# A first layer norm of two row groups computed one stage earlier, and fewer spare matrix products at the start of the next stage

## What is computed

```python
def _layernorm(x, axis=-1, eps=1e-05):
    m = jnp.mean(x, axis=axis, keepdims=True)
    v = jnp.var(x, axis=axis, keepdims=True)
    return (x - m) / jnp.sqrt(v + eps)

# sublayer 1: state-space layer (a scan over time), then residual and norm
x = _layernorm(x + _L0_attn_ref(x, ...), axis=-1)
# sublayer 2: x1 = _ln(x, ln1_g, ln1_b), then self attention on x1
x = _layernorm(x + _L0_xattn_ref(x, ctx_512, ...), axis=-1)

def _ln(x, g, b):
    m = jnp.mean(x, -1, keepdims=True)
    v = jnp.var(x, -1, keepdims=True)
    return (x - m) * jax.lax.rsqrt(v + 1e-05) * g + b
...
x = _ln(xx, ln1_g, ln1_b)          # the norm that the change moves for 8 of 64 sequences
x = x + _mha(x, x, ...)            # which begins with xn = _ln(x, lnx_g, lnx_b)
```

## Time and profile before

| | us |
|---|---|
| median of 3 runs | 3524.48 |
| lowest, highest | 3520.35, 3525.49 |
| the profiled execution: its own time | 3520.38 |
| its span in the trace | 3518.5 |
| PE busy | 3132.9 (89%) |
| DVE, ACT, POOL busy | 2410.5, 1967.9, 2064.2 |
| mean granted TensorE clock | 0.959 of full speed |

### The profile page before, as it was taken

The page is one execution under the profiler, slowest core; times in us unless marked ns, Lnnn a source line. Parts: engine busy times, 40 slices in busy tenths (PEclk is TensorE's granted clock), DMA queues, the critical chain, the costliest instruction groups (busy, mean ns, idle before and its releaser), DMA issues. The chain is left out here.

```text
span 3518.5 us, 101747 instructions
## 1 busy us (share of the span) xinstructions
PE 3132.9 (89%) x40973; PEld 1931.2 (55%) x40973; DVE 2410.5 (69%) x5699; ACT 1967.9 (56%) x3510; POOL 2064.2 (59%) x1842
## 2 busy tenths in 40 slices
PE   6888888877999999898999999999999989999676
PEld 2433444433555556665666666665555545666575
DVE  5999999994555555585665556677888855666465
ACT  5666666652566666432666654335555536666354
POOL 5888888884787877663111114556777742343365
PEclk8999999998999999998999998999999989999798
DMA  4222222225600000000000000000000000000364
GB/s 143 103 90 91 96 100 92 89 88 195 217 2 2 2 2 2 16 1 13 4 5 5 5 3 6 8 8 2 2 2 2 2 17 24 21 17 14 98 175 116
DMA packets 50327, 165.42 MB, mean 47 GB/s; under 512 B 11822, under 2 KB 23217, under 8 KB 40784
## 3 DMA queue, kind: packets, MB, share of 16 engines
q1 hardware_dynamic: 45520, 150.43, 13.1%
q0 software_dynamic: 4352, 8.47, 0.7%
HBM read 149.89 MB, written 43.65 MB: 55 GB/s over the span
## 5 line engine op out<-in xcount | busy, mean ns | idle before, releaser
L530 DVE TENSOR_TENSOR_SCAN XC<-ssm_dA,ssm_db 128x2048 f32<-128x2048 f32 x128 | 565.2, 4416 | 55.6 <-PE ssm_db L374 55.6
L479 ACT ACTIVATE ssm_dA<-ssm_delta,ssm_nega 128x508 f32<-128x508 f32 x512 | 326.0, 707 | 165.9 <-DVE XC L530 162.6
L1229 POOL TENSOR_TENSOR self_pm<-self_pT,weights 128x512 f32<-128x512 f32 x256 | 322.6, 1294 | 54.4 <-ACT self_pT L953 53.0
L594 POOL TENSOR_TENSOR XC<-XC,XB 128x1536 f32<-128x1536 f32 x64 | 253.3, 3958 | 87.9 <-DVE XC L530 87.9
L1235 POOL TENSOR_TENSOR XC<-XC,XB 128x128 f32<-128x128 f32 x128 | 58.5, 458 | 391.6 <-DVE XB L1111 391.6
L594 POOL TENSOR_TENSOR ssm_hC<-XC,XB 128x1536 f32<-128x1536 f32 x64 | 251.8, 3934 | 36.6 <-DVE XC L530 36.6
L374 PE MATMUL ssm_db<-XB,ssm_dxT 32*128 32x128 f32 x4096 | 157.0, 292 | 103.3 <-DVE XC L530 88.9
L374 PEld LDWEIGHTS ssm_db<-XB,ssm_dxT 32*128 32x128 f32 x4096 | 131.7, 193 | 203.8 <-DVE XC L530 183.9
L1097 DVE TENSOR_REDUCE self_nmax<-self_scores 128x4 f32<-128x512 f32 x256 | 158.0, 679 | 82.0 <-PE self_scores L830 81.8
L2663 POOL TENSOR_TENSOR XC<-XC,weights 128x512 f32<-128x512 f32 x128 | 161.8, 1285 | 73.1 <-ACT XC L2497 73.1
L2671 POOL TENSOR_TENSOR XC<-XC,weights 128x512 f32<-128x512 f32 x128 | 161.4, 1283 | 49.7 <-ACT XC L2506 49.5
(11 more groups left out here) (454 smaller groups left out, 8354.3 us busy)
## 6 DMA issues: line engine op xcount, KB each, us to landing
XB<-c_rows SPq DMA_DIRECT2D x64, 1024.0 KB
sorted<-in_padding SPq DMA_DIRECT2D x1, 33280.0 KB, 109.2
experts_we<-in_w_experts SPq DMA_DIRECT2D x72, 323.0 KB, 3.1
experts_rt<-sorted SPq DMA_DIRECT2D x72, 65.0 KB
ssm_xT<-in_xT SPq DMA_DIRECT2D x16, 256.0 KB
XC<-in_w_experts SPq DMA_DIRECT2D x9, 256.0 KB
weights<-in_w_self SPq DMA_DIRECT2D x1, 1412.0 KB, 7.3
cross_ctx_t<-in_ctx SPq DMA_DIRECT2D x16, 77.0 KB
```

The source lines that it names most:

```text
L479: o = act.activation(dA[:, p % 2, :].rearrange("p (b k t) -> p b k t", b=GROUP, k=4)[:, :, k, 1:T], by_batch(delta[:, slot, half, :])[:, : ...
L530: dve.tensor_tensor_scan(states(p).rearrange("p m t -> p (m t)"), dA[:, p % 2, :], db[:, :], 0.0, ALU.mult, ALU.add).then_inc(h_ready, 1)
L594: pool.tensor_tensor(weighted(p).rearrange("p (b k) t -> p b k t", k=4)[:, :, 0:3, :], states(p).rearrange("p (b k) t -> p b k t", k=4)[:, ...
L1229: pool.tensor_tensor(pm[:, n % 2, r, :].rearrange("p (h t) -> p h t", h=4), pT[:, n % 2, r, :].rearrange("p (h t) -> p h t", h=4), bcast(V ...
```

## The change

In the last step of the state-space phase, where the group index is NG, three pieces are added. DVE takes the row statistics of X for groups 0 and 1 (`next_rows`, part 0). ACT normalises these rows from X into XC (`next_norm`, part 0) once the last readers of XC's states are done. POOL computes the reciprocal deviations and shifts and applies gain and offset (`next_inverse`, `next_spread`, part 1). In self attention the same work is taken out for groups 0 and 1, and each engine raises the semaphores by the amount that the removed work raised. The spare products ahead of the transposes go from 9 to 2, and those ahead of the first q product from 2 to 1.

```diff
@@ ssm_phase, ACT, in step(g, slot) @@
                         elif more(g):
                             decay(g + 1, 1 - slot, 0)
+                    elif p == 0:
+                        next_norm()
...
+            def next_norm():
+                act.wait_ge(hC_dve, NG * U)
+                act.wait_ge(hC_pool, NG * U)
+                for n in range(2):
+                    act.wait_ge(next_step, 4 * n + 4)
+                    for b in range(GROUP):
+                        o = act.activation(XC[:, n * GROUP + b, :], X[:, n * GROUP + b, :], ACT.Identity,
+                                           scale=next_rstd[:, n, b:b + 1], bias=next_shift[:, n, b:b + 1])
+                    o.then_inc(next_normed, 1)
@@ ssm_phase, DVE @@
+                    if p == 0 and not there(g):
+                        next_rows()
...
+            def next_rows():
+                dve.wait_ge(x_out, 2)
+                for n in range(2):
+                    row_stats(dve, lambda b: X[:, n * GROUP + b, :], next_stats[:, n], next_mv[:, n], next_vec, n * VEC, mark)
@@ ssm_phase, POOL @@
+                    if p == 1 and not there(g):
+                        pool.wait_ge(env["weights"]["self"][1], 16)
+                        for n in range(2):
+                            next_inverse(n)
+                        for n in range(2):
+                            next_spread(n)
...
+            def next_inverse(n):
+                pool.wait_ge(next_vec, (n + 1) * VEC)
+                pool.sem_inc(mark, 1)
+                inv_std(pool, power[:, :], next_mv[:, n], next_rstd[:, n], next_step, 4 * n)
+                pool.wait_ge(next_step, 4 * n + 2)
+                pool.tensor_tensor(next_shift[:, n], next_mv[:, n, :, 0], next_rstd[:, n], ALU.mult).then_inc(next_step, 1)
+                pool.wait_ge(next_step, 4 * n + 3)
+                pool.sem_inc(mark, 1)
+                pool.tensor_scalar(next_shift[:, n], next_shift[:, n], -1.0, None, ALU.mult).then_inc(next_step, 1)
+
+            def next_spread(n):
+                gain, offset = env["self_vectors"]
+                rows = XC[:, n * GROUP:(n + 1) * GROUP, :]
+                pool.wait_ge(next_normed, n + 1)
+                pool.sem_inc(mark, 1)
+                pool.tensor_tensor(rows, rows, bcast(gain, 1, GROUP), ALU.mult).then_inc(next_step, 1)
+                pool.wait_ge(next_step, 2 * n + 9)
+                pool.sem_inc(mark, 1)
+                pool.tensor_tensor(rows, rows, bcast(offset, 1, GROUP), ALU.add).then_inc(next_step, 1)
@@ wide_attention_phase, PE @@
-            keep_warm(pe, ob, ident, 9 if own else 3)
+            keep_warm(pe, ob, ident, 2 if own else 3)
...
-                        keep_warm(pe, ob, ident, 2)
+                        keep_warm(pe, ob, ident, 1)
@@ wide_attention_phase, ACT @@
             if own:
-                x1_norm(0)
+                act.sem_inc(x1_normed, 2)
                 in_norm(0)
-                x1_norm(1)
@@ wide_attention_phase, DVE @@
             if own:
-                x1_stats(0)
+                dve.sem_inc(vec, 2 * GROUP)
+                in_stats(0)
...
             dve.tensor_copy(pick[:, :, :], bcast(sel, 2, P)).then_inc(folded, 1)
...
             dve.memset(nsplit[:, :, :], 0.0).then_inc(folded, 1)
-            if own:
-                in_stats(0)
-            else:
+            if not own:
...
             if own:
-                x1_stats(1)
+                dve.wait_ge(vec, VEC)
+                dve.sem_inc(vec, 2 * GROUP)
             in_stats(1)
@@ wide_attention_phase, POOL @@
             if own:
-                x1_inv(0)
-                x1_spread(0)
+                pool.sem_inc(pool_step, 5)
+                pool.sem_inc(x1_ready, 1)
             in_inv(0)
             if own:
-                x1_inv(1)
-                x1_spread(1)
+                pool.wait_ge(pool_step, POOL)
+                pool.sem_inc(pool_step, 5)
+                pool.sem_inc(x1_ready, 1)
             in_inv(1)
```

6 lines of the change are left out of this document (added).

## The result

The changed kernel takes 3511.63 us, median of nine runs (3501.21 to 3516.74). The kernel before, measured beside it, takes 3521.94, also of nine (3512.50 to 3525.91). The ratio of the two is 0.9972, with a 95% interval of 0.9960 to 0.9984: 9.9 us faster, between 5.6 and 14.1. The forecast was 3511.6, 12.9 us faster. Time and sign were right, and the gain came out some 3 us smaller than forecast, a difference that lies inside the interval. That the forecast time was hit to 0.03 us is luck: the forecast started from 3524.48 for the kernel before, whose median of nine is 2.5 us lower, and this made up for the smaller gain.

What follows compares the result with a forecast made beforehand. At the seam into self attention, the first norm through DVE's queue and then spare products delay PE in series. Starting the first q product 12.9 us earlier, all else zero, gives 3524.48 - 12.9 = 3511.6 us, range 3504 to 3519.5.

Steps and rivals of the forecast that it cites:

- What bounds the seam: Start of self attention: first norm through DVE's queue up to 841.91, then spare products, in series set the first q product.
- Part 1: Last state-space step: added DVE, POOL and ACT work hidden in idle time, phase end unmoved; POOL overrun 0, range 0 to 2.1 us.
- POOL still in the gain and offset when DVE's last statistics are done: Last state-space step: a sign, named beforehand, that would show the forecast wrong.
- Part 2: Start of self attention: without the norm, bias copies start behind PE's product, spare products at 836.16 instead of 841.91, 5.75 us.
- Part 3: Fewer spare products: first q product at 840.8 or 841.45 against 854.12, 13.3 or 12.7 us earlier; 12.9 taken.
- my bounds of 3.25 and 4.51: Delay in us from the start of dense PE work to the rise of the granted clock, read from two places.
- The low level did not reach q and k: Rival at the q and k products: low clock through all eight costs 6.9 us, products before 0.8; 3519.3; chance 0.10.
- The slower case: Rival in the first attention beats: PE stays at 1.2 GHz, loss 20.1 us with group 1, 3531.7; chance 0.04.
- Only the spare products count: Rival at the seam: PE doesn't wait for the first norm, fewer spare products alone give 6.9 us, 3517.6; chance 0.03.
- The clock doesn't fall at the seam: Rival at the barrier: clock stays up, first q product at 838.4, 15.7 us earlier, 3508.8; chance 0.05.
- Part 4: Attention loop after the first q product: earlier start carries through; low clock stretches plus or minus 3.2 us, taken as zero.
- The sum: Whole kernel: median 3524.48 - 12.9 = 3511.6 us, profiled execution 3507.5 us.

Runs made afterwards that it cites:

- norm_only: The change with nine and two spare products as before, so only the norm is moved: median 3517.76 us, ratio 0.9992 to before.
- products_only: The kernel before with two and one spare products instead of nine and two, norm not moved: median 3515.36 us, ratio 0.9990.
- changed: First profiled execution of the changed kernel, with no further edit: 3516.01 us; median of the kernel 3511.63 us, ratio 0.9972 to before.
- changed_again: The changed kernel once more without edit, for a second profile: profiled 3500.75 us, median 3511.18 of 12, ratio 0.9977 to before.
- tail_only: The change with eight instead of six spare products at the end of the state-space phase: median 3504.37 us, ratio 0.9968 to before.
- tail_two_late: The change with eight spare products in the tail, and DVE applying the second group's gain and offset after POOL's last norm: median 3502.22 us, ratio 0.9955.
- tail_eight: The change with the second group's gain and offset on DVE, eight spare products in the tail, none at the start: median 3500.62 us, ratio 0.9946.
- pad_late: The change with the 33 MB padding transfer issued after the sixteenth sequence's score products: median 3509.73 us, ratio 0.9974 to before.

## Why the prediction was right, step by step

**What bounds the seam: right, with one wait overlooked.** Two things stood in series, the norm through DVE's queue and the spare products. Removing one alone brings the first beat forward by 4.8 or 4.6 (`norm_only`), 3.3 or 4.9 (`products_only`), both by 11.4. That spare products also covered ACT's copy behind the second group's norm was not in the forecast; the change takes this wait away by its other half, which was luck.

**Part 1, POOL: the term was zero where it depends on the clock.** I set its overrun at 0, with 0 to 2.1 kept. POOL's times were right, but not the time at which DVE would want it. When the last products run at the higher level (3.66 us) the inverse is 1.4 us late (`changed`); at the lower one (5.34) it is on time (`changed_again`). One of my own signs of being wrong, POOL still in the gain and offset when DVE's last statistics are done, so appeared in that trace. Besides, 0.4 us went at the barrier, which I had not foreseen. The price of both can be read. Timelines of DVE and PE, before, and of DVE, changed:

```profile
805.99 4.42 DVE L530 TENSOR_TENSOR_SCAN XC<-ssm_dA,ssm_db 128x2048 f32<-128x2048 f32 x1 [0.57 <-PE ssm_db L374]
814.55 5.90 PE L389 MATMUL ssm_y<-ssm_hC,weights 64*64 64x512 f32 x32 [5.04 <-POOL ssm_hC L594]
```

```profile
804.81 4.42 DVE L547 TENSOR_TENSOR_SCAN XC<-ssm_dA,ssm_db 128x2048 f32<-128x2048 f32 x1 [1.48 <-PE ssm_db L379]
```

From the start of the last scan to the barrier, less the time of the last products, it is 19.2 us before (831.09 - 805.99 - 5.90), and the same in the three other traces with the old tail. It is 21.0 in `changed` (829.44 - 804.81 - 3.66) and in the two others whose POOL was late, and 19.6 in `changed_again` (832.74 - 807.79 - 5.34) and the three others where it was on time. So the term cost 1.8 or 0.4 us, inside the 0 to 2.1 that I kept.

**Part 2, the bias products: the mis-sized term.** I took L762 to end 4.05 us after PE's start as before, so the copies at 835.3, 4.1 behind the barrier. The copies came at 835.06, but only because the barrier was earlier. Measured from it, L812 ended 5.6 us behind it (832.97 + 2.06 - 829.4), instead of 4.15 (before). PE had stood idle for 3.97 us at the barrier instead of 2.21, 2.60 in `changed_again`, and the clock fell within a microsecond of the barrier, not after 1.6. Stretch of the changed kernel:

```profile
829.00:830.00 1.00, 0.44 (x3) 0.47 (x3) 0.12 (x1) 0.48 (x1) 0.10 (x1) 0.74 0.03 8
```

All the one-column products then run at the lower level. That is 1.4 us and makes the step from 12.9 to 11.4 in this trace. In `changed_again` the clock fell 0.7 us behind the barrier, the bias products cost 0.9 us more than forecast, and the late rise of the clock the other 0.5. With two more products ahead of the barrier it comes back: `tail_only` and `tail_two_late` have first beats 1.7 and 1.6 us earlier than the change, and in `tail_eight` the bias products end 3.0 us behind the barrier.

**Part 3, fewer spare products: right in the steps, helped by luck in the times, and one bound too narrow.** Spare products at 835.94 (forecast 836.2), transposes at 839.51 (839.6), the first q product at 841.00 (840.8 to 841.5), the first scores at 849.51 (849.3 to 850). These times agree because the barrier came 1.7 us earlier, which hides the 1.4 of part 2. From the first spare to the first q product it was 5.06 us, within my 4.6 to 5.3. The clock rose 3.8 us after the spare products began, between my bounds of 3.25 and 4.51:

```profile
839.00:840.00 1.00, 1.00 (x5) 0.48 (x4) 0.00 (x0) 0.00 (x0) 0.92 (x2) 0.64 1.29 426
```

In `changed_again` it rose after 5.0 us, above the upper bound, and 5.57 us lay between the two. Two values were too few to bound a delay that differs from execution to execution.

**The rivals.** The low level did not reach q and k: 3.92 us for eight records of q, as before (3.85). With no spare products at all it did, and cost 1.5 us (2.8 in `tail_eight`), not 6.9. The page of the Trainium skill that I had set against the change, "TensorE: Matmul & The Clock Gate", asks in its section "Why this matters for your kernels" to keep TensorE busy without a break for full throughput. The three spare products that are left were enough for that here. The slower case, the low level through the first beats, did not come: the clock was at 1.00 from 839.7 to 860.2 in the changed kernel. "Only the spare products count" fell with `products_only`: its 6.9 us would have been 3.3 to 4.9, for ACT's queue was in the way. "The clock doesn't fall at the seam" did not happen either in the change; the three kernels with eight products in the tail come near to it.

**Part 4, carrying through: right in the mean, and the spread was real.** The loop kept 12.50 and 11.77 of its lead. I allowed plus or minus 3.2 for low stretches. Between the first and the eleventh beat the leads grew by up to 2.3 us (`tail_eight`) and shrank by up to 4.4 (`norm_only`), so the allowance was near the truth. But I had put it down to the clock only. The stops of PE of up to 3.1 us during the transfer are the other part, and stood in the trace of before (2.20 at 902.49).

**The sum.** Self attention became 12.4 us shorter in one trace and 11.7 in the other (624.0 less 611.6 and 612.3), against 12.9. The state-space phase varies by itself: with its old code it took 829.9 to 831.8 in four traces (mean 830.8), with the change's code 829.4 to 834.3 in six (mean 832.2). The means differ by 1.4 us, less than twice what four and six values so scattered leave uncertain. Part 1 shows what the change does there: 0.4 or 1.8 us more behind the last scan. What differs ahead of the scan is code that the change leaves alone. My forecast was that the phase would end where it did. The barrier behind self attention came 14.1 us earlier in one trace (1441.0) and 10.1 in the other (832.7 + 612.3 = 1445.0). The median says 9.9, interval 5.6 to 14.1. The 0.4 or 1.8 us of the tail would explain most of the 2 us between this and the shorter self attention, but this is not shown, since later phases vary by more (`cross` 525.4 to 533.7, `narrow` 441.9 to 452.6 over all traces).

The best version by its median is `tail_eight`, 0.9946 (0.9930 to 0.9962) of before, about 19 us. It is clearly faster than before. Against the change (0.9960 to 0.9984 in one comparison, 0.9964 to 0.9989 in the other) the intervals just overlap or just don't, and the two never ran beside each other, so an advantage of some 10 us is likely but not shown. The traces account for 3 to 4 us of it in self attention (608.8 against 611.6 and 612.3), and the first beat for less than 1.

## What to carry to other kernels

Spare products and a serial chain that cover each other must be removed together, and whatever else they covered has to be looked for on every engine's queue: here a copy on ACT behind another group's norm. Count times at a seam from the barrier: the times on the trace's own clock agreed with the forecast by the luck of an early barrier. Look at what TensorE did ahead of it. Its idle time there is not all that decides at which level the first products run: `tail_only` idled 2.27 us and `products_only` 2.21, yet the clock fell 3.1 and 0.9 us behind the barrier, with eight and six products in the tail. Compare phases, not whole traces, when an effect is 0.3%: unchanged phases differed by 8 to 11 us.

## What the runs showed of the hardware that was not expected

- During a large transfer (33 MB, DMA share about 1.0) and just at its end TensorE stands for 0.2 to 3.1 us at a time with nothing that the profile shows to wait for; when the transfer was issued later, the stops came later (0.21 and 2.56 us in `pad_late`). They stand at places of TensorE's instruction list that lie multiples of 256 records apart. Stops of up to 0.7 us stand elsewhere too, at a smaller DMA share (before, 0.69 at 3275.5, share 0.20).
- Two more wide products ahead of a barrier held the granted clock at 1.00 until 3.1 to 3.9 us behind it, over products of one column; with the shorter row and 3.97 us of idling it fell within 0.1 us of the barrier.
- POOL's instructions of 0.23 and 1.04 us took 0.44 and 1.56 beside DVE products that read two operands from SBUF.
- POOL's time between its last norm and its first instruction behind the barrier is 2.86 to 2.88 us in three kernels and 3.21 to 3.28 in seven that hold the moved norm; three unused semaphores do not do it, and the cause is open.
